# Second attention: the mask added by VectorE in the pass that finds the row maximum, instead of by a matmul

## The chip, the cores and the metric

One core of a Trainium2 chip. The time is the device time of one execution in microseconds; a lower one is better. The median of three runs stands for the kernel. Names: TensorE is PE in the rows (PEld its weight loads), VectorE is DVE, ScalarE is ACT, GpSimd is POOL, SyncE is SP.

## The reference, cut to what matters

A block of four parts on x of 16 x 256 tokens x 256: a cross attention with rotary positions, a mixture of experts, a second cross attention with a mask, and a quantised feed-forward part. The change lies in the second attention, 16 heads of 64, 256 queries and 256 keys per batch:

```python
scores = jnp.einsum('bhqd,bhkd->bhqk', q, k) / jnp.sqrt(jnp.float32(d))
scores = jnp.where(mask == 0, jnp.float32(-1000000000.0), scores)
probs = jax.nn.softmax(scores, axis=-1)
out = jnp.einsum('bhqk,bhkd->bhqd', probs, v)
```

The mask is one row of 256 keys for each query; it is the same for all heads.

## The kernel before

All parts run one after the other; the second attention (`attention1`, from L856) takes from about 1190 to 2043 us of the profile. Each engine has a program of its own, written out by hand, and semaphores join them; each engine runs its instructions in order.

**Batches and stages.** For each of the 16 batches the front makes the inputs, keys, queries and values of the batch (matmuls into the two banks pF, then high and low f16 halves: for queries and values ScalarE writes the high half, QN[0] at L1212 and VH at L1220, and VectorE the low half, L1322 and L1330; for the inputs L1205 and L1306; for keys VectorE takes the sum out of PSUM at L1315 and GpSimd splits it). The SyncE queue stacks the halves into QS, KD2 and KZ. The back works through 16 units. A unit u is a pair of heads (u // 2) and one half of the queries (u % 2), so its scores are 128 queries x 2 heads x 256 keys, one PSUM bank.

**A unit before.** TensorE (`scores`, L1133): a matmul of the identity with the mask, in bf16 and 512 columns wide, opens the bank (L1142), and four matmuls add the products of the f16 halves (L1145, L1146). VectorE (`maxima`, L1336): one reduction over the bank gives the two negated maxima NM (L1338). ScalarE (`exps`, L1225): two activations take the exponential from the bank to P32 with NM as bias, each followed by a read of its accumulator, the row sum SM (L1229). VectorE takes the reciprocal RS (L1342), GpSimd normalises P32 (L1060), TensorE transposes it (L1154) into pT, ScalarE writes the high half PH (L1238) and VectorE the low half PL (L1348), and TensorE multiplies with the values (L1167, bank pO) and with the output weights (L1179, bank pG). The output of a pair goes out of pO in halves by L1243 and L1353.

**Order.** The batch is cut into 16 turns, and a turn holds what each engine does between two units. `step` (L948) sets it: in each turn first the old batch's remainders, then the new unit's early part, then its late part, then the front of the next batch and the adding up of the experts' rows (`comb`). Lags: scores, maxima and exponentials of u in turn u, reciprocal and normalising in u + 1, transposes and halves in u + 3, the product with the values of pair p in 2p + 6, the output product in 2p + 8, the end of the batch in turn 23, that is 7 of the next. On ScalarE a turn is: high half of P (u - 3), output half, exponentials of u, then the front's item. On VectorE: maximum of u, reciprocal of u - 1, low half of u - 3, output half in even turns, then the front's item, then `comb`. The front's items come in these turns (of VectorE and ScalarE): inputs 2; keys 2, 4, 5, 6; queries 8, 9, 10, 12; values 13, 14 and 0, 1 of the next batch. In turn 0 VectorE also normalises the inputs (L1300), in turn 7 it writes the result (L1357, L1361), in 4, 6, 10 and 13 it adds experts' rows. The mask of a batch is made by GpSimd in turn 13 of the batch before (L1051).

**Buffers and waits.** Two banks pS, two pT, four P32, NM, SM and RS. Scores of u wait for the exponentials of u - 2, which free the bank (L1140); the exponentials wait for the transposes of u - 4, which free P32 (L1227); TensorE waits for the mask at unit 0 (L1136). Batches 1 to 14 run in a loop of two batches per turn (`batches`, L946), so every second batch ends at a loop wrap. The last batch has no front beside it.

Of the kernel before, what the change touches and what calls it, by code (L numbers as in the profile page):

```python
# [855 lines left out]
def attention1(nc, ctx, X, XW, ctxT_d, mask_d, bias_d, consts, POS, GW, y_d):  # L856
# [9 lines left out]
    SHRINK = float(dh) ** -0.5  # L866
    MASKED = -2.0 ** 40
# [103 lines left out]
    with nc.Block() as block:  # L971
# [35 lines left out]
        def _(pool):  # L1007
# [24 lines left out]
            def front(b, par):  # L1032
# [14 lines left out]
                def make_mask():  # L1047
                    mask_in.wait(pool, b, 16)
                    s_full.wait(pool, b, 1 - UNITS) if not isinstance(b, int) or b > 1 else None
                    nc.gpsimd.nop(nofuse=True)  # L1050
                    nc.gpsimd.tensor_scalar(maskq[par][:], maskin[:], 0.0, MASKED, ALU.is_equal, ALU.mult).then_inc(masks.sem, 1)  # L1051
# [14 lines left out]
        def _(pe):  # L1066
# [65 lines left out]
            def back(b, par):  # L1132
                def scores(u):  # L1133
                    p2, j = u // 2, u % 2
                    if u == 0:
                        masks.wait(pe, b, 1)  # L1136
                        stacked[0].wait(pe, b, 160)
                    if u == UNITS // 2:
                        stacked[1].wait(pe, b, 160)
                    e_ready.wait(pe, b, u - 1) if u or not isinstance(b, int) or b else None  # L1140
                    out = pS[u % 2]
                    nc.tensor.matmul(out[:], identb[:], maskq[par][:, j:j + 1, :].broadcast_to([P, 2, S]), start=True, stop=False)  # L1142
                    for a in range(2):
                        q = QS[par][a][:, p2, j * P:(j + 1) * P]
                        nc.tensor.matmul(out[:, a, :], q, KD2[par][a][:, p2, :], start=False, stop=False)  # L1145
                        last = nc.tensor.matmul(out[:, a, :], q, KZ[par][a][:, p2, :], start=False, stop=(a == 1))  # L1146
                    last.then_inc(s_full.sem, 1)
# [42 lines left out]
        def _(act):  # L1190
            act.wait_ge(consts_in, 64)
            nc.scalar.activation(bvh[:], bvt[:], ACT.Copy).then_inc(folds, 1)
            nc.scalar.activation(bqk[:, 0, :], bqk[:, 0, :], ACT.Copy, scale=float(dh) ** -0.5).then_inc(folds, 1)
# [30 lines left out]
            def back(b, par):  # L1224
                def exps(u):  # L1225
                    s_max.wait(act, b, u + 1)
                    t_full.wait(act, b, u - 3) if u > 2 or not isinstance(b, int) or b else None  # L1227
                    for a in range(2):
                        last = nc.scalar.activation(P32[u % 4][:, a, :], pS[u % 2][:, a, :], ACT.Exp, bias=NM[u % 4][:, a:a + 1],  # L1229
# [20 lines left out]
        def _(dve):  # L1250
# [84 lines left out]
            def back(b, par):  # L1335
                def maxima(u):  # L1336
                    s_full.wait(dve, b, u + 1)
                    nc.vector.tensor_reduce(NM[u % 4][:], pS[u % 2][:], AX.X, ALU.max, negate=True).then_inc(s_max.sem, 1)  # L1338
# [1132 lines left out]
```

## Time and profile before

| | us |
|---|---|
| median of 3 runs | 2278.15 (2271.85 to 2279.02) |
| the profiled execution | 2261.47 |
| its span, first to last instruction | 2259.8 |
| busy in it: PE / DVE / ACT / POOL | 1749.2 / 1442.3 / 1076.2 / 1019.9 |

Three views are used: busy time of the engines in a stretch, the waits (an engine's line, the line that released it, total, count and longest), and the timeline (start, duration, engine, line, output and inputs; in brackets the idle time just before and its releaser). Durations of neighbouring instructions on one engine may overlap, so the time that one holds its engine is read from the start of the next. A row with x2 is two instructions merged.

### The profile page before, as it was taken

How to read it: one execution, taken by the hardware profiler on the slowest of the kernel's cores; microseconds unless marked ns; L12 is line 12 of the kernel's file. 1: busy time of each engine (PE TensorE's matmuls, PEld its weight loads, DVE VectorE, ACT ScalarE, POOL GpSimd, SP SyncE). 2: the span in 40 equal slices, each digit the busy share in tenths (PEclk: the TensorE clock that was granted, in tenths of full speed). 3: DMA queues.
4: the chain of work that ended last, by engine and by line, in shares of the span. 5: the costliest groups of instructions: out<-in, count | busy, mean ns of one | idle time of the engine just before them, and what ended most of it. 6: DMA issues, size and time to landing. Idle time of an engine off the chain costs nothing. (4 is left out here: it accounts for less than half of the span.)

```text
span 2259.8 us, 45795 instructions
## 1 busy us (share of the span) xinstructions
PE 1749.2 (77%) x14311; PEld 1163.0 (51%) x14312; DVE 1442.3 (64%) x2962; ACT 1076.2 (48%) x2519; POOL 1019.9 (45%) x1471
## 2 busy tenths in 40 slices
PE   0588888882382689999995899999999989992375
PEld 0344444441240355666663676777666667771123
DVE  4356666666961244444444777777777777876797
ACT  1266666663520122222221666666666666671464
POOL 1655665522717102232324666665665566640005
PEclk9699999995586799999997999999999999995598
DMA  3000000003700001222213222333232222311002
GB/s 103 10 11 11 10 10 10 10 1 104 223 2 0 1 24 54 67 71 68 71 51 91 69 67 70 80 80 77 72 78 75 67 69 69 76 34 39 0 0 75
DMA packets 91476, 118.43 MB, mean 52 GB/s; under 512 B 18465, under 2 KB 60857, under 8 KB 91321
## 3 DMA queue, kind: packets, MB, share of 16 engines
q1 hardware_dynamic: 76216, 90.16, 14.9%
q0 software_dynamic: 8576, 17.87, 2.9%
q10 hardware_dynamic: 6528, 8.39, 1.1%
q8 instruction: 90, 1.47, 0.3%
q14 instruction: 66, 0.53, 0.1%
HBM read 56.40 MB, written 17.90 MB: 33 GB/s over the span
## 5 line engine op out<-in xcount | busy, mean ns | idle before, releaser
L1060 POOL TENSOR_SCALAR a_P<-a_P,a_RS 128x256 f32<-128x256 f32 x512 | 255.6, 499 | 239.1 <-DVE a_RS L1342 209.7
L1229 ACT ACTIVATE a_P<-a_pS,a_NM 128x256 f32<-128x256 f32 x512 | 237.8, 471 | 203.7 <-DVE a_NM L1338 203.2
L814 DVE TENSOR_REDUCE a_M<-a_pS 128x2 f32<-128x512 f32 x256 | 164.7, 685 | 147.1 <-PE a_pS L625 146.7
L1338 DVE TENSOR_REDUCE a_NM<-a_pS 128x2 f32<-128x512 f32 x256 | 174.7, 682 | 30.9 <-PE a_pS L1146 28.0
L1238 ACT ACTIVATE a_PH<-a_pT 128x512 f16<-128x512 f32 x256 | 154.1, 602 | 74.6 <-PE a_pT L1154 63.9
L1348 DVE TENSOR_TENSOR a_PL<-a_pT,a_PH 128x512 f16<-128x512 f32 x256 | 172.4, 673 | 13.5 <-ACT a_PH L1238 13.4
L1154 PE MATMUL a_pT<-g_ident,a_P 128*128 128x128 f32 x1024 | 156.0, 275 | 23.9 <-POOL a_P L1060 21.5
L753 ACT ACTIVATE a_PT<-a_pT 128x512 f32<-128x512 f32 x256 | 139.0, 597 | 71.6 <-PE a_pT L644 71.4
L1154 PEld LDWEIGHTS a_pT<-g_ident,a_P 128*128 128x128 f32 x1024 | 119.9, 141 | 42.5 <-POOL a_P L1060 19.4
L1921 ACT ACTIVATE me_hh<-me_pH 128x512 f16<-128x512 f32 x72 | 43.0, 597 | 175.7 <-PE me_pH L1908 156.2
L1145 PE MATMUL a_pS<-a_KD,a_QS 128*128 128x256 f16 x512 | 126.4, 274 | 0.0
L1146 PE MATMUL a_pS<-a_KZ,a_QS 128*128 128x256 f16 x512 | 126.4, 274 | 0.0
L99 PE MATMUL a_pF<-a_ch,xw_XW 128*128 128x256 f16 x512 | 100.2, 280 | 30.5 <-DVE a_VL L1330 26.6
L1966 DVE TENSOR_TENSOR me_h<-me_SG,me_pU 128x512 f32<-128x512 f32 x72 | 49.5, 688 | 98.6 <-PE me_pU L99 93.9
L99 PE MATMUL me_pG<-mo_w1h,me_xt 128*128 x288 | 98.7, 384 | 7.0 <-issue 7.0
L1229 ACT ACTIVATION_READ_ACCUMULATOR a_P<-a_pS,a_NM 128x1 f32 x512 | 102.3, 200 | 0.0
L99 PE MATMUL a_pF<-a_xh,xw_XW 128*128 128x256 f16 x512 | 99.1, 273 | 2.2 <-DVE a_k L1315 1.1
L1142 PE MATMUL a_pS<-a_maskq,g_identb 128*128 128x512 bf16 x256 | 97.8, 382 | 2.1 <-DMA a_QS<-a_QN 1.5
L99 PE MATMUL me_pU<-mo_w3h,me_xt 128*128 x288 | 98.4, 383 | 0.0
L1179 PE MATMUL a_pG<-xw_XW,a_oh 128*128 128x256 f16 x512 | 93.4, 278 | 5.5 <-DVE a_proj L1357 4.6
L1837 POOL DMA_INDIRECT me_xg<-rows,me_idx x72 | 70.3, 976 | 54.5 <-POOL me_idx L1834 34.6
L1322 DVE SCALAR_TENSOR_TENSOR a_QN<-a_pF,a_bqk,a_QN 128x256 f16<-128x256 f32 x128 | 56.0, 479 | 57.2 <-ACT a_QN L1212 44.8
(421 smaller groups left out, 5218.3 us busy)
## 6 DMA issues: line engine op xcount, KB each, us to landing
a_KD<-a_KN SPq DMA_DIRECT2D x128, 128.0 KB
a_QS<-a_QN SPq DMA_DIRECT2D x128, 128.0 KB
mr_stage<-mw SPq DMA_DIRECT2D x24, 512.0 KB, 4.7
ys<-me_yb SPq DMA_DIRECT2D x72, 128.0 KB
a_ctxin<-ctxT SPq DMA_DIRECT2D x32, 256.0 KB, 2.8
a_KZ<-a_KN SPq DMA_DIRECT2D x64, 128.0 KB
g_X<-x SPq DMA_DIRECT2D x1, 4096.0 KB, 14.8
rows<-mr_row ACTq DMA_DIRECT2D x32, 128.0 KB, 3.7
```

The costliest lines, as they stand in the source:

```text
L99: last = nc.tensor.matmul(out, a(kt), b(kt), start=(n == 0), stop=(n == 3 * chunks - 1))
L753: nc.scalar.activation(PT[(2 * p2 + a) % 8][:], pT[a][:], ACT.Exp, scale=float(dh) ** -0.5).then_inc(p_ready.sem, 1)
L814: nc.vector.reduce_max(M[:, :, a, p2], pS[a][:], AX.X).then_inc(s_max.sem, 1)
L1060: last = nc.gpsimd.tensor_scalar(P32[u % 4][:, a, :], P32[u % 4][:, a, :], RS[u % 4][:, a:a + 1], LIFT, ALU.mult, ALU.mult)
L1142: nc.tensor.matmul(out[:], identb[:], maskq[par][:, j:j + 1, :].broadcast_to([P, 2, S]), start=True, stop=False)
L1145: nc.tensor.matmul(out[:, a, :], q, KD2[par][a][:, p2, :], start=False, stop=False)
L1146: last = nc.tensor.matmul(out[:, a, :], q, KZ[par][a][:, p2, :], start=False, stop=(a == 1))
L1154: last = nc.tensor.transpose(pT[u % 2][:, a, kt, :], P32[u % 4][:, a, kt * P:(kt + 1) * P], ident[:])
L1229: last = nc.scalar.activation(P32[u % 4][:, a, :], pS[u % 2][:, a, :], ACT.Exp, bias=NM[u % 4][:, a:a + 1], accum_out=SM[u % 4][:, a:a + 1])
L1238: nc.scalar.activation(PH[p2 % 2][:, :, :, j * P:(j + 1) * P].rearrange("p a k q -> p (a k) q"), pT[u % 2][:].rearrange("p a k q -> p (a k ...
L1338: nc.vector.tensor_reduce(NM[u % 4][:], pS[u % 2][:], AX.X, ALU.max, negate=True).then_inc(s_max.sem, 1)
L1348: nc.vector.tensor_tensor(PL[p2 % 2][:, :, :, j * P:(j + 1) * P].rearrange(f), pT[u % 2][:].rearrange(f), PH[p2 % 2][:, :, :, j * P:(j + 1 ...
```

## The change

TensorE no longer adds the mask; the first product opens the bank. The sign of the scaled queries is turned (SHRINK, and the scale of their bias), so the bank holds negated scores, and the mask is +2^40 where it was -2^40. VectorE runs one `tensor_tensor_reduce` for each of the two heads of a unit: it adds the mask to 256 columns of the bank, writes the sum to P32 and its minimum, which is the negated maximum of the scores, to NM. ScalarE reads P32 and writes the exponentials over it, with a scale of -1. The bank is free when the second pass is done, so the scores of u wait for the maxima of u - 2. The waits for the mask and for P32 go to VectorE, which gets a no-operation that carries them. GpSimd's wait before it overwrites a mask goes by the maxima.

```diff
-    SHRINK = float(dh) ** -0.5
-    MASKED = -2.0 ** 40
+    SHRINK = -float(dh) ** -0.5
+    MASKED = 2.0 ** 40
...
                 def make_mask():
                     mask_in.wait(pool, b, 16)
-                    s_full.wait(pool, b, 1 - UNITS) if not isinstance(b, int) or b > 1 else None
+                    s_max.wait(pool, b, -UNITS) if not isinstance(b, int) or b > 1 else None
...
                 def scores(u):
                     p2, j = u // 2, u % 2
                     if u == 0:
-                        masks.wait(pe, b, 1)
                         stacked[0].wait(pe, b, 160)
                     if u == UNITS // 2:
                         stacked[1].wait(pe, b, 160)
-                    e_ready.wait(pe, b, u - 1) if u or not isinstance(b, int) or b else None
+                    s_max.wait(pe, b, u - 1) if u or not isinstance(b, int) or b else None
                     out = pS[u % 2]
-                    nc.tensor.matmul(out[:], identb[:], maskq[par][:, j:j + 1, :].broadcast_to([P, 2, S]), start=True, stop=False)
                     for a in range(2):
                         q = QS[par][a][:, p2, j * P:(j + 1) * P]
-                        nc.tensor.matmul(out[:, a, :], q, KD2[par][a][:, p2, :], start=False, stop=False)
+                        nc.tensor.matmul(out[:, a, :], q, KD2[par][a][:, p2, :], start=(a == 0), stop=False)
...
-            nc.scalar.activation(bqk[:, 0, :], bqk[:, 0, :], ACT.Copy, scale=float(dh) ** -0.5).then_inc(folds, 1)
+            nc.scalar.activation(bqk[:, 0, :], bqk[:, 0, :], ACT.Copy, scale=-float(dh) ** -0.5).then_inc(folds, 1)
...
                 def exps(u):
                     s_max.wait(act, b, u + 1)
-                    t_full.wait(act, b, u - 3) if u > 2 or not isinstance(b, int) or b else None
                     for a in range(2):
-                        last = nc.scalar.activation(P32[u % 4][:, a, :], pS[u % 2][:, a, :], ACT.Exp, bias=NM[u % 4][:, a:a + 1],
+                        last = nc.scalar.activation(P32[u % 4][:, a, :], P32[u % 4][:, a, :], ACT.Exp, bias=NM[u % 4][:, a:a + 1], scale=-1.0,
                                                     accum_out=SM[u % 4][:, a:a + 1])
...
                 def maxima(u):
                     s_full.wait(dve, b, u + 1)
-                    nc.vector.tensor_reduce(NM[u % 4][:], pS[u % 2][:], AX.X, ALU.max, negate=True).then_inc(s_max.sem, 1)
+                    if u == 0:
+                        masks.wait(dve, b, 1)
+                    t_full.wait(dve, b, u - 3) if u > 2 or not isinstance(b, int) or b else None
+                    nc.vector.nop(nofuse=True)
+                    for a in range(2):
+                        last = nc.vector.tensor_tensor_reduce(P32[u % 4][:, a, :], pS[u % 2][:, a, :], maskq[par][:, u % 2, :], 1.0, 3.0e38,
+                                                              ALU.add, ALU.min, NM[u % 4][:, a:a + 1])
+                    last.then_inc(s_max.sem, 1)
```

## Rows read from the trace of the kernel before

**Rows 1.** Busy us (and counts) of PE, PEld, DVE, ACT, POOL; clock, DMA share, GB/s.
```profile
1340.00:1940.00 600.00, 551.74 (x4847) 422.47 (x4846) 468.71 (x1101) 381.86 (x1193) 367.46 (x563) 0.99 0.30 73
```

**Rows 2.** Waits in 1340 to 1940 us: total us, times, longest.
```profile
ACT a_P L1229 <- DVE a_NM L1338: 159.0, 150, 2.1
...
DVE a_VL L1330 <- ACT a_VH L1220: 36.2, 46, 1.0
DVE a_QN L1322 <- ACT a_QN L1212: 33.6, 35, 1.2
...
DVE a_NM L1338 <- PE a_pS L1146: 21.1, 17, 2.5
...
PE a_pF L99 <- DVE a_VL L1330: 20.9, 12, 2.2
```

**Rows 3.** Timeline of DVE, turn 9 of a batch.
```profile
1677.11 0.68 DVE L1338 TENSOR_REDUCE a_NM<-a_pS 128x2 f32<-128x512 f32 x1
1677.71 0.15 DVE L1342 RECIPROCAL a_RS<-a_SM 128x2 f32<-128x2 f32 x1
1677.78 0.67 DVE L1348 TENSOR_TENSOR a_PL<-a_pT,a_PH 128x512 f16<-128x512 f32 x1
1679.61 0.88 DVE L1322 SCALAR_TENSOR_TENSOR a_QN<-a_pF,a_bqk,a_QN 128x256 f16<-128x256 f32 x2 [1.16 <-ACT a_QN L1212]
1680.40 0.68 DVE L1338 TENSOR_REDUCE a_NM<-a_pS 128x2 f32<-128x512 f32 x1
```

**Rows 4.** Timeline of ACT in the same turn.
```profile
1677.82 0.48 ACT L1229 ACTIVATE a_P<-a_pS,a_NM 128x256 f32<-128x256 f32 x1 [0.87 <-DVE a_NM L1338]
1678.19 0.19 ACT L1229 ACTIVATION_READ_ACCUMULATOR a_P<-a_pS,a_NM 128x1 f32 x1
...
1678.64 0.20 ACT L1229 ACTIVATION_READ_ACCUMULATOR a_P<-a_pS,a_NM 128x1 f32 x1
1678.74 0.84 ACT L1212 ACTIVATE a_QN<-a_pF,a_bqk 128x256 f16<-128x256 f32 x2
```

**Rows 5.** Timeline of PE: mask matmul and the next one; a resumption at a loop wrap.
```profile
1657.00 0.38 PE L1142 MATMUL a_pS<-a_maskq,g_identb 128*128 128x512 bf16 x1
1657.22 0.27 PE L1145 MATMUL a_pS<-a_KD,a_QS 128*128 128x256 f16 x1
...
1696.36 1.02 PE L1154 MATMUL a_pT<-g_ident,a_P 128*128 128x128 f32 x4 [2.38 <-POOL a_P L1060]
```

**Rows 6.** Timeline of DVE, turns 4 to 6.
```profile
1661.59 0.69 DVE L1338 TENSOR_REDUCE a_NM<-a_pS 128x2 f32<-128x512 f32 x1 [1.07 <-PE a_pS L1146]
...
1662.66 0.69 DVE L1348 TENSOR_TENSOR a_PL<-a_pT,a_PH 128x512 f16<-128x512 f32 x1 [0.30 <-ACT a_PH L1238]
1663.27 0.41 DVE L1353 SCALAR_TENSOR_TENSOR a_ol<-a_pO,a_oh 128x256 f16<-128x256 f32 x1
1663.60 0.87 DVE L1315 TENSOR_SCALAR a_k<-a_pF,a_bqk 128x256 f32<-128x256 f32 x2
...
1669.02 0.88 DVE L1315 TENSOR_SCALAR a_k<-a_pF,a_bqk 128x256 f32<-128x256 f32 x2 [0.53 <-PE a_pF L99]
```

**Rows 7.** Timeline of DVE: the maxima of turn 11 and of turn 13.
```profile
1684.08 0.68 DVE L1338 TENSOR_REDUCE a_NM<-a_pS 128x2 f32<-128x512 f32 x1
...
1689.04 0.68 DVE L1338 TENSOR_REDUCE a_NM<-a_pS 128x2 f32<-128x512 f32 x1
```

**Rows 8.** Groups by line, 1340 to 1940 us: busy us, mean ns; idle time before.
```profile
L1201 ACT ACTIVATE a_ch<-a_ctxin 128x512 f16<-128x512 f32 x12 | 7.7, 639 | 0.0
L1205 ACT ACTIVATE a_xh<-a_pF 128x512 f16<-128x512 f32 x12 | 7.1, 593 | 0.0
```

**Rows 9.** The maxima: ns min/median/max, first and last start; turn 0 of two batches.
```profile
L1338 DVE TENSOR_REDUCE a_NM<-a_pS x256: 670/680/693, 1240.2 to 2032.7; 128x2 f32<-128x512 f32 x128
...
1700.81 0.69 DVE L1338 TENSOR_REDUCE a_NM<-a_pS 128x2 f32<-128x512 f32 x1 [2.37 <-PE a_pS L1146]
...
1751.25 0.69 DVE L1338 TENSOR_REDUCE a_NM<-a_pS 128x2 f32<-128x512 f32 x1
```

## The prediction

> **What bounds the kernel now.** I read the windows first: in 1340 to 1940 us, the middle of the second attention, TensorE is busy 551.7 of 600 us, VectorE 468.7, ScalarE 381.9, GpSimd 367.5 [rows 1]. Taken alone that says TensorE is the bound, and taking a matmul from it should pay. So the next view was who waits for whom [rows 2]. TensorE's gaps end with VectorE's work (L1330, 20.9 us in 12 waits), while VectorE waits for ScalarE (36.2 us for VH, 33.6 us for QN) and ScalarE for VectorE's maxima (159.0 us). VectorE waits for TensorE's scores only 21.1 us in 17 waits. Two engines that wait for each other on every turn are a loop, so I read their timelines through one turn.
>
> A turn is one unit u of the program. In turn 9, VectorE finds the maximum at 1677.11, takes the reciprocal and the low half of P, and then stands idle 1.16 us until ScalarE has the high half of the queries; at 1679.61 it takes the low half and at 1680.40 the next maximum [rows 3]. ScalarE starts the exponentials at 1677.82, 0.71 after the maximum began; they and the two accumulator reads take 0.92, and QN follows at 1678.74 with no gap [rows 4]. The turn is 0.71 + 0.92 + 0.87 (QN with the hand-over) + 0.79 = 3.29 us, and 1680.40 - 1677.11 is 3.29. TensorE is not in that loop. By the plans, eight of the sixteen turns of a batch have a ScalarE item of the front (inputs, queries or values) that VectorE must follow and are of this kind: 0, 1, 2, 8, 9, 10, 13, 14. Turns 11 and 12 are one loop too: 4.96 us from maximum to maximum with two sets of exponentials in it [rows 7]. Turns 5, 6, 7 and 15 are filled by VectorE itself, apart from 0.53 us at L1315. Turns 3 and 4 hang on TensorE: the maximum waits 1.07 us for the scores, L1348 then 0.30 us for the transposes [rows 6]. A batch without a loop wrap is 50.4 us (1751.25 - 1700.81) [rows 9].
>
> **The change, part by part** (per batch of 16 units; 15 batches run with a front beside them).
>
> Mask matmul gone: the next matmul starts 0.22 us after it [rows 5], so TensorE gets 16 x 0.22 = 3.5 us back per batch. It counts only where TensorE is what the loop waits for: once in turns 3 and 4 (-0.22).
>
> Maximum in two passes. Now one pass starts the next instruction 0.60 us later (1677.11 to 1677.71) and lasts 0.68 [rows 3, 9]. The new operation isn't in the trace. Its nearest pass is L1353, 128x256 from PSUM with an immediate: 0.41 us long, next instruction 0.33 after its start [rows 6]. It also writes out its minimum. VectorE shows no such write; its nearest row is the reciprocal of 128x2, which lasts 0.15 and lets the next start after 0.07 [rows 3]. I take these, with 0.08 for the second figure: the engine is held 2 x (0.33 + 0.08) = 0.82 us, +0.22 against 0.60; the result is there after 0.33 + 0.08 + 0.33 + 0.15 = 0.89 us, +0.21 against 0.68. Low end: no cost for the minimum, 0.33 + 0.41 = 0.74 (+0.06), engine +0.06. High end: nothing overlaps, the minimum costs ScalarE's 0.20 and the no-operation that carries the waits 0.07, so 0.07 + 2 x (0.41 + 0.20) = 1.29 (+0.61), engine +0.7. I take the middle values because they come from the same engine's own rows.
>
> The Trainium skill (VectorE: DVE Perf Modes, section "Two Vector instructions with no wait between them") says that an operation which writes its accumulator is two instructions, and its Vector Engine (DVE) Microarchitecture Reference, section 5.2, gives 1.04 ns per column and some 75 ns per instruction after overlap. Estimated from that page alone, the four would hold the engine 0.83 us. No run here shows it yet.
>
> Exponentials from SBUF: ScalarE's 128x512 copy takes 0.639 us from SBUF (L1201) and 0.593 from PSUM (L1205) [rows 8], +0.046 per instruction, +0.09 per unit. The sign in the scale is an immediate and free.
>
> Bank free earlier (scores wait for the maximum of u-2, not its exponentials): worth nothing, TensorE hardly waits there; the cover is that it reaches scores after its own queue. Waits moved to VectorE: t_full of u-4 stands in TensorE's queue ahead of scores u, so it has passed when s_full has; the mask is made on GpSimd in turn 13, three turns ahead. Behind a wait there would queue the reciprocal, the low half and all front items, and behind them TensorE; I see none that lasts. GpSimd's mask instruction is the same; negated queries cost nothing.
>
> **The sum.** The eight loop turns: each +0.21 + 0.09 = +0.30, 2.40. Turns 11 and 12: +0.21 and twice 0.09, +0.39. Turns 7 and 15, VectorE full: +0.22 each, 0.44. Turns 5 and 6: twice 0.22, less the 0.53 wait at L1315 that fills up, as TensorE is now early: -0.09. Turns 3 and 4: -0.22; VectorE's longer pass fits in its 1.07 us wait. Together +2.92 us per batch, x15 = +43.8. At some wraps of the batch loop TensorE resumes late (2.38 us of idle time) and VectorE's maximum then waits 2.37 us for it [rows 5, 9]; there turns 14 and 15 give and take nothing. Of the 17 waits of 21.1 us [rows 2], 12 are turn 4's 1.07, and the 8.3 us left are some four such wraps: -2. The last batch has no front and is set by TensorE at one place and VectorE at the next: 0. **+42 us.** The profiled execution took 2261.5 us around a span of 2259.8, below the three runs shown (2271.9 to 2279.0). On its own time the sum gives 2303.5; on the median of 2278.15 it gives **2320**, which I forecast.
>
> Same sum with the low ends: 8 x 0.15 + 0.24 + 0.12 - 0.41 - 0.22 = +0.9 per batch, +14 us, 2292. With the high ends: 8 x 0.70 + 0.8 + 1.4 + 0.9 + 0.1 = +8.8, +132 us, 2410.
>
> **Rivals.** *TensorE is the bound* (the other side): at 92% busy, with the matmul's time coming back on every unit, 256 x 0.22 = 56 us less, 2222. It decides if in turns 8 to 14 TensorE's queries or values were what ScalarE waits for. Against it: QN starts the moment the exponentials end [rows 4], and TensorE is found waiting for VectorE and GpSimd [rows 2]. The Trainium skill (Trainium Kernel Development and Optimization, section "Performance Expectations") calls matmul busy time a bad metric for how close a kernel is to its limit; by that rule the trace agrees, its 92% standing beside those waits. Chance 0.08. If TensorE bounded part of the turns only, some gain would be left after the VectorE cost.
>
> *The passes overlap wholly*, and an early TensorE also cures part of the stalls at the wraps: +14 less some 10, within 0.3% (2271.3 to 2285.0, about what a measurement of this kernel can tell from no change). Chance 0.08.
>
> *The passes run one after the other*, each waiting for its minimum: VectorE goes from 39.1 us per 50 (468.7 of 600) [rows 1] to over 50 and is the bound in every turn: up to 2410. For it: an unseen operation, on 512 instructions; against it: all VectorE rows overlap by 0.07 to 0.09. Chance 0.2.
>
> *The change doesn't do what it says* in one point: the bank is released earlier, and nobody was waiting for it. That is in the forecast already and has no chance of its own. The forecast itself has 0.64.
>
> **Numbers.** Slower: 0.64 + 0.20, so 0.84; same 0.08; faster 0.08. The range leaves out the faster rival and the upper half of the serial one: 2286 to 2362.
>
> **What would show it.** Right: no L1142; two passes of 0.40 to 0.45 us per unit with a second row each; exponentials some 0.05 us longer; VectorE busy up by about 3.5 us per batch; turn 9 at 3.6 us; ScalarE still waits for NM in most units; TensorE busy near 85% and its waits for VectorE and GpSimd up. Its granted clock, 0.99 in the window [rows 1], could fall with longer gaps, which would add to the time. Wrong: if turn 9 stays at 3.29, the passes are cheaper than any row says; if the batch falls below 50 us, TensorE was in the loop; if t_full or the mask shows up as a releaser of VectorE, the moved waits are not free.

## The result and the profile after

| | us |
|---|---|
| before, median of 4 runs | 2275.0 (2269.6 to 2279.0) |
| after, median of 4 runs | 2312.26 (2307.6 to 2320.5) |
| ratio, with its 95% interval | 1.0169 [1.0131, 1.0208] |
| span of the profiled execution, before / after | 2259.8 / 2310.4 |

The change costs 37 us by the medians; 42 were forecast. To see where the time went, I took the starts of the maxima of all 256 units from VectorE's timeline in both traces; from one start to the next is a turn. Over the 15 batches that have a front beside them, the turns add up to +41.7 us, against a forecast of +43.8 - 2. The two profiled spans differ by more, 50.6 us; 7.6 of that lies behind the last maximum, nearly all in work that the change doesn't touch, and over all the traces of this case that tail takes 227 to 239 us with and without the change. The batch loop has five wraps: it runs batches 1 to 12 in six passes of two, and the last batches stand behind it. Sorted by turn:

| turns, 15 batches | forecast | after | what it is |
|---|---|---|---|
| 8 to 14 | +28.4 | +16.3 | loop turns, and 11 with 12 |
| 0 to 7 | +12.2 | +8.1 | loop turns 0 to 2; 3 to 6; 7 |
| 15, no wrap behind it | +3.3, with wraps | +5.4 | end of a batch |
| 15, at the 5 wraps | -2 | +11.8 | loop wraps |

(The forecast's figures are its per-batch terms times 15: 8 to 14 are five turns of 0.30 and the 0.39; 0 to 7 are 0.90 - 0.22 - 0.09 + 0.22.) The total is right because two errors nearly cancel: the turns grew by less than forecast, and the wraps of the batch loop grew where I had a small gain.

The busy window that answers to [rows 1], with the same columns:

```profile
1340.00:1940.00 600.00, 508.11 (x4372) 386.37 (x4372) 462.45 (x1568) 371.40 (x1128) 344.22 (x531) 0.96 0.28 69
```

TensorE has gone from 551.7 to 508.1 us of 600, and the kernel is slower. VectorE's busy time even fell in the window, for the window now holds less of the work; in it its instructions rose from 1101 to 1568. The granted clock fell from 0.99 to 0.96.

The page's groups and the source view of the new line show its price; the columns are busy us, mean ns, idle time before, and then ns min/median/max with the first and last start:

```profile
L1340 DVE CUSTOM_DVE_ANT_0 a_P<-a_pS,a_maskq 128x256 f32<-128x256 f32 x512 | 194.9, 417 | 49.9 <-PE a_pS L1144 44.9
```

```profile
L1340 DVE DVE_READ_ACCUMULATOR2_ANT a_NM<- x512: 72/82/86, 1241.3 to 2076.4; 128x1 f32 x171
```

Turn 9 on VectorE, which answers to [rows 3]:

```profile
1701.33 0.41 DVE L1340 CUSTOM_DVE_ANT_0 a_P<-a_pS,a_maskq 128x256 f32<-128x256 f32 x1
1701.67 0.08 DVE L1340 DVE_READ_ACCUMULATOR2_ANT a_NM<- 128x1 f32 x1
1701.67 0.42 DVE L1340 CUSTOM_DVE_ANT_0 a_P<-a_pS,a_maskq 128x256 f32<-128x256 f32 x1
1702.01 0.08 DVE L1340 DVE_READ_ACCUMULATOR2_ANT a_NM<- 128x1 f32 x1
1702.01 0.16 DVE L1346 RECIPROCAL a_RS<-a_SM 128x2 f32<-128x2 f32 x1
...
1703.98 0.88 DVE L1319 SCALAR_TENSOR_TENSOR a_QN<-a_pF,a_bqk,a_QN 128x256 f16<-128x256 f32 x2 [1.22 <-ACT a_QN L1210]
1704.77 0.41 DVE L1340 CUSTOM_DVE_ANT_0 a_P<-a_pS,a_maskq 128x256 f32<-128x256 f32 x1
```

Read the starts. The read of the minimum and the second pass both start at 1701.67, the second read and the reciprocal both at 1702.01: the read takes no time of its own from the engine. The two passes hold it 0.68 us (1701.33 to 1702.01), against 0.60 for the one before. The turn is 1704.77 - 1701.33 = 3.44, against 3.29.

ScalarE in the same turn, answering to [rows 4]:

```profile
1702.13 0.51 ACT L1226 ACTIVATE a_P<-a_P,a_NM 128x256 f32<-128x256 f32 x1 [1.14 <-DVE a_NM L1340]
1702.55 0.19 ACT L1226 ACTIVATION_READ_ACCUMULATOR a_P<-a_P,a_NM 128x1 f32 x1
1702.64 0.49 ACT L1226 ACTIVATE a_P<-a_P,a_NM 128x256 f32<-128x256 f32 x1
...
1703.13 0.81 ACT L1210 ACTIVATE a_QN<-a_pF,a_bqk 128x256 f16<-128x256 f32 x2
```

The exponentials start 0.80 after the maximum (0.71 before) and take 1.00 until QN (0.92 before); QN with the hand-over takes 0.85 (0.87), and VectorE's QN 0.79 (0.79). So 0.80 + 1.00 + 0.85 + 0.79 = 3.44. The loop is the one that the prediction read out, with two terms longer by 0.09 and 0.08.

Waits in the same window, answering to [rows 2]:

```profile
ACT a_P L1226 <- DVE a_NM L1340: 188.1, 142, 2.7
...
PE a_pT L1152 <- POOL a_P L1060: 56.0, 51, 2.9
...
DVE a_QN L1319 <- ACT a_QN L1210: 43.4, 44, 1.2
DVE a_P L1340 <- PE a_pS L1144: 36.5, 24, 4.0
DVE a_VL L1327 <- ACT a_VH L1218: 36.3, 45, 1.0
```

TensorE's time went into waiting: it waits 56.0 us for normalised P. New, though, is VectorE's wait for scores, up from 21.1 us to 36.5, with single waits of up to 4.0 us. The longest, 3.86 to 3.99 us, stand at the five loop wraps. TensorE's timeline and VectorE's at the wrap before the batch of 1727.59:

```profile
1724.98 0.27 PE L1144 MATMUL a_pS<-a_KZ,a_QS 128*128 128x256 f16 x1
```

```profile
1723.56 0.16 DVE L1287 TENSOR_TENSOR a_rstd<-a_root,a_corr 128x2 f32<-128x2 f32 x1
1727.59 0.42 DVE L1340 CUSTOM_DVE_ANT_0 a_P<-a_pS,a_maskq 128x256 f32<-128x256 f32 x1 [3.86 <-PE a_pS L1144]
```

The last product of unit 0's scores ends at 1725.25, and VectorE starts on them at 1727.59, 2.3 us later (0.8 to 3.3 us at the five wraps). The wait is put down to TensorE because that signal is the last one the profile shows; but TensorE had been done. Before, at the wrap of [rows 9], VectorE's maximum started right behind the scores. Turn 15 before a wrap is now 6.19, 6.26, 6.15, 6.14 and 6.18 us, where it was 4.67, 4.29, 2.69, 4.54 and 2.94. The spread of before follows TensorE's granted clock: in the 4 us ahead of the maximum it is 0.57, 0.58 and 0.61 at the three long wraps (the lower of the two levels, 1.2 GHz, reads 0.50), and 1.00 at the two short ones:

```profile
1696.81:1700.81 4.00, 4.00 (x27) 2.54 (x26) 1.53 (x8) 1.89 (x6) 0.96 (x2) 0.61 0.04 10
1798.32:1802.32 4.00, 2.88 (x28) 2.19 (x29) 2.68 (x8) 1.92 (x6) 1.83 (x4) 1.00 0.13 45
```

Against those two, a wrap has grown by 3.4 us, not by the 2.4 of the mean.

### The profile page after: what moved, and what is told of

It is laid out like the page before. It is cut to its first block and busy times, and to the rows that moved or that the text cites. A ratio compares the mean times of both kernels' runs of the same rounds, so it can differ in the third digit from the quotient of the medians.

```text
span 2310.4 us, 46083 instructions
## 1 busy us (share of the span) xinstructions
PE 1741.2 (75%) x14047; PEld 1152.3 (50%) x14056; DVE 1467.7 (64%) x3730; ACT 1092.3 (47%) x2519; POOL 1018.6 (44%) x1471
## 5 line engine op out<-in xcount | busy, mean ns | idle before, releaser
L1226 ACT ACTIVATE a_P<-a_P,a_NM 128x256 f32<-128x256 f32 x512 | 255.7, 500 | 254.4 <-DVE a_NM L1340 252.2
L1340 DVE CUSTOM_DVE_ANT_0 a_P<-a_pS,a_maskq 128x256 f32<-128x256 f32 x512 | 194.9, 417 | 49.9 <-PE a_pS L1144 44.9
L1152 PE MATMUL a_pT<-g_ident,a_P 128*128 128x128 f32 x1024 | 163.1, 283 | 74.0 <-POOL a_P L1060 69.7
L99 PE MATMUL a_pF<-a_ch,xw_XW 128*128 128x256 f16 x512 | 105.1, 289 | 37.4 <-DVE a_VL L1327 31.7
L1226 ACT ACTIVATION_READ_ACCUMULATOR a_P<-a_P,a_NM 128x1 f32 x512 | 95.7, 187 | 0.0
L1573 POOL DMA_INDIRECT slots<-ms_tok,g_POS x64 | 61.9, 967 | 61.6 <-DVE g_POS L1711 42.4
```

The costliest lines, as they stand in the source:

```text
L99: last = nc.tensor.matmul(out, a(kt), b(kt), start=(n == 0), stop=(n == 3 * chunks - 1))
L1152: last = nc.tensor.transpose(pT[u % 2][:, a, kt, :], P32[u % 4][:, a, kt * P:(kt + 1) * P], ident[:])
L1226: last = nc.scalar.activation(P32[u % 4][:, a, :], P32[u % 4][:, a, :], ACT.Exp, bias=NM[u % 4][:, a:a + 1], scale=-1.0, accum_out=SM[u % ...
L1340: last = nc.vector.tensor_tensor_reduce(P32[u % 4][:, a, :], pS[u % 2][:, a, :], maskq[par][:, u % 2, :], 1.0, 3.0e38, ALU.add, ALU.min, N ...
```

## The experiments

Three theories were at stake. *Loop*: the turns are set by the VectorE-ScalarE loop, and grow by the pass and by the source. *TensorE*: its time matters too, through its idle gaps or its clock. *Restart*: VectorE comes back late at a wrap because of what its program has become. All ratios are against runs of the kernel before on the same chip.

### TensorE's time alone: the mask matmul taken out

```diff
-                        masks.wait(pe, b, 1)
-                    nc.tensor.matmul(out[:], identb[:], maskq[par][:, j:j + 1, :].broadcast_to([P, 2, S]), start=True, stop=False)
-                        nc.tensor.matmul(out[:, a, :], q, KD2[par][a][:, p2, :], start=False, stop=False)
+                        nc.tensor.matmul(out[:, a, :], q, KD2[par][a][:, p2, :], start=(a == 0), stop=False)
```

The mask isn't applied.

> The kernel before with the mask matmul left out and nothing put in its place (the mask is not applied). The loop theory (VectorE's maximum, ScalarE's exponentials and high half, VectorE's low half, next maximum set the turn; TensorE only waits): turn 9 stays at 3.29 us and the maxima of a batch stay near 50.4 us; between 10 us less and 15 us more than before, that is 2265 to 2290. More is possible where TensorE, done sooner, idles longer at the end of a batch and its clock is granted low after it, which the changed kernel shows (2.41 us idle at 1667.19, then matmuls 0.21 us apart where they are 0.11 apart elsewhere). The TensorE theory: 256 x 0.22 us less, 2219.

Measured: 2268.46 us, ratio 0.999 [0.9977, 1.0003]. The window:

```profile
1340.00:1940.00 600.00, 529.86 (x4634) 404.54 (x4635) 471.71 (x1098) 379.48 (x1192) 366.64 (x565) 0.97 0.29 72
```

TensorE has 22 us less in 600, and the time is the same; turn 9 stays at 3.29. Turn 3 is mostly 2.20 for 2.41, the 0.22 that was forecast for turns 3 and 4, but three batches have 3.14 to 3.18 there, with a granted clock of 0.80 to 0.88 in that turn, and the five wraps add next to nothing either way (3.96 in the mean, before 3.83). The rival in which TensorE is the bound is dead.

### The other way round: a blank matmul put into the changed kernel

```diff
+    blank = s.sb("blank", [P, 1, S], BF16)
...
+                    nc.tensor.matmul(out[:], identb[:], blank[:, 0:1, :].broadcast_to([P, 2, S]), start=True, stop=False)
```

> The changed kernel with a matmul of the same width as the mask's, identity times a tile of zeros, put back in front of the products (it adds zero). The loop theory: TensorE has the time to spare; its idle gap before turn 0 shortens and its clock stays high there, so 0 to 10 us less than the changed kernel, 2302 to 2312. The TensorE theory: 56 us more than the changed kernel, 2368.

Measured: 2314.6, ratio 1.0208 [1.0186, 1.0231]; the change itself has 1.0169 [1.0131, 1.0208]. Turn 9 is 3.44, and turn 15 at the wraps 6.18, 6.37, 6.45, 6.15 and 6.15: giving TensorE its old load back cures nothing. So the long wraps don't come from a TensorE that is less busy. Nor do they come from its clock: at the third and fourth of these wraps it is 1.00 in the 4 us ahead of the maximum, as it is at all five of the fourth experiment (6.55 to 6.81 us). The 0 to 10 us less that I expected didn't come either: the turns add up to 7.9 us more than with the change, 7.3 of them in turns 0 to 7, where turn 3 takes 3.2 to 3.7 us in seven batches.

### The waits and the no-operation alone

```diff
                     s_full.wait(dve, b, u + 1)
+                    if u == 0:
+                        masks.wait(dve, b, 1)
+                    t_full.wait(dve, b, u - 3) if u > 2 or not isinstance(b, int) or b else None
+                    nc.vector.nop(nofuse=True)
                     nc.vector.tensor_reduce(NM[u % 4][:], pS[u % 2][:], AX.X, ALU.max, negate=True).then_inc(s_max.sem, 1)
```

> The kernel before with only the three things that the change puts in front of the maxima on VectorE: the wait for the mask at unit 0, the wait for the transposes of u-4, and the no-operation. In the changed kernel VectorE restarts 3.9 us after its last instruction at each of the five wraps of the batch loop (turn 15 takes 6.2 us where it took 2.7 to 4.7), and turns 7 and 13, where VectorE waits for itself, are longer by 0.27. If the added instructions do this: turn 15 at the wraps goes to some 5 to 6 us, turns 7 and 13 up by 0.1 to 0.2, 10 to 20 us more than before, 2285 to 2295. If they are free and the wraps come from TensorE's clock or from the passes: 2275 within 5.

Measured: 2275.33, ratio 1.0029 [1.0014, 1.0044]. Turns 8 and 9 stay at 3.30 and 3.29, so in a loop turn the waits are free. They are not where short instructions stand ahead of the maximum: turn 6 is 4.39 for 4.19, turn 13 4.45 for 4.35 and turn 15 2.54 for 2.31. Turns 0 to 7 carry +8.8 us of the turns' sum of +8.7, and the wraps, at 2.95 to 3.24 us, give 3.8 back. In both of these figures TensorE's clock has a part. Turn 3 is 2.51 for 2.41, but 3.2 to 3.7 in five batches, and in three of them turn 2 is longer too, 6.0 us together; there the granted clock falls to 0.50 for some 2 us in turns 2 and 3, behind an idle gap of TensorE of 2.0 to 2.2 us that other batches have at the full clock, while it reads 1.00 in those turns of before in every batch but the first. At the wraps it is the other way round: all five have 1.00 here, and three of before had 0.57 to 0.61, some 5 us. The two nearly cancel, so that moving the waits costs some 7 us in all (2275.33 against 2268.3), a term that I had at nothing. Whether the waits also bring on the low clock isn't shown; three batches of the first experiment have it in turn 3 without them. The opposite, the change without these waits or the no-operation, wasn't tried.

### The maximum ahead of the front's item, in every turn

If the loop sets the turns, taking its hinge out should pay: VectorE takes the maximum of u + 1 before it waits for ScalarE's half of QN or VH.

```diff
-                return {}, plan(*[(u, lambda u=u: maxima(u)) for u in range(UNITS)], ...
+                return {}, plan((0, lambda: maxima(0)), ...
+                            *[(u - 1, lambda u=u: maxima(u)) for u in range(1, UNITS)], (END, finish))
```

> The changed kernel with VectorE's two passes of unit u+1 put in front of the front's item of turn u instead of behind it (turns 1 to 15), so that ScalarE can go from the high half straight to the next exponentials. The loop theory: the loop is cut; ScalarE's own work per turn is 2.1 to 2.5 us and TensorE's 2.7, so turn 9 falls from 3.44 to under 3 and a batch from 53 to 45 to 48 us: 2200 to 2250. The TensorE theory, and the theory that VectorE's own work bounds the changed kernel: the order of VectorE's queue moves nothing, 2312 within 10.

Measured: 2310.73, ratio 1.0203 [1.0169, 1.0238]. No gain in the total, where 2200 to 2250 was expected, though turn 9 falls to 2.14. Turns 8 to 15 take 24.1 us for 26.2, but turns 0 to 7 take 27.7 for 26.2, and a wrap 6.7. The waits show what replaced the loop where it hadn't been the limit:

```profile
DVE a_P L1340 <- PE a_pS L1144: 119.1, 102, 3.2
POOL a_KN L1043 <- DVE a_k L1312: 61.5, 22, 4.3
```

In turns 0 to 7 VectorE now stands in front of scores that aren't there yet, with the keys' item queued behind it, on which GpSimd waits. The order pays in the late turns only.

### The maximum ahead in six turns only, without and with the change

```diff
+    EARLY = (9, 10, 11, 13, 14, 15)
...
-                return {}, plan(*[(u, lambda u=u: maxima(u)) for u in range(UNITS)], ...
+                return {}, plan(*[(u, lambda u=u: maxima(u)) for u in range(UNITS) if u not in EARLY], ...
+                            *[(u - 1, lambda u=u: maxima(u)) for u in EARLY], (END, finish))
```

> The kernel before with the maxima of units 9, 10, 11, 13, 14 and 15 put in front of the front's item of the turn ahead, so that the loop is cut in the turns of the queries and values alone. In the run that moved all maxima, turns 0 to 7 became longer (27.7 us where the changed kernel has 26.2: its keys hang on VectorE) and turns 8 to 15 shorter (24.1 against 26.2). The loop theory: turns 8 to 15 fall from 25.2 to 23 to 24.5 us per batch and the rest stays, 10 to 30 us less than before, 2240 to 2260. If TensorE is at its bound there: nothing, 2268.

> The same order in the changed kernel. The loop theory: turns 8 to 15 near the 24.1 us of the full reorder, turns 0 to 7 near 26.2, so 2 us per batch or 30 us less than the changed kernel, 2275 to 2290, the wraps still near 6 us. If the changed kernel is bound by the number of its VectorE instructions: 2312 within 8.

Measured: the kernel before, reordered, 2236.15, ratio 0.9862 [0.9838, 0.9885]; the changed one, reordered, 2240.5, ratio 0.9881 [0.9859, 0.9903]. The first one's window:

```profile
1340.00:1940.00 600.00, 568.07 (x5038) 437.26 (x5037) 484.61 (x1147) 403.21 (x1245) 383.48 (x585) 1.00 0.30 75
```

This shows the loop: not one instruction is taken away, turn 9 falls from 3.29 to 2.05, and every engine is busier. (A single turn now overstates it, since the starts of the maxima have moved: outside the wraps turns 8 to 15 together fall from 24.6 to 23.0 us.) With the loop cut, the two ratios lie within each other's intervals. The changed kernel came out below the 2275 to 2290 expected, because that expectation took turns 8 to 15 from the run that had moved all maxima; moving six gives 21.8 us there and not 24.1. Outside the wraps the turns of the changed one are 42.3 us shorter than those of the kernel before, and of the unchanged one 33.4: the longer pass and the slower source cost nothing there any more. What is left of the change's price is in the wraps, 7.26, 6.94, 8.00, 6.75 and 8.50 us with it, 4.48 to 5.01 without; this is more than the 6 us expected, and why they grew with the new order is open (at the 8.00 and the 8.50 the scores end only 0.3 us before VectorE takes them, with a granted clock of 0.60 and 0.50 ahead of them).

### One pass for both heads

```diff
-                    for a in range(2):
-                        last = nc.vector.tensor_tensor_reduce(P32[u % 4][:, a, :], pS[u % 2][:, a, :], ...
+                    last = nc.vector.tensor_tensor_reduce(P32[u % 4][:], pS[u % 2][:], maskq[par][:, u % 2:u % 2 + 1, :].broadcast_to([P, 2, S]), 1.0, 3.0e38,
+                                                          ALU.add, ALU.min, NM[u % 4][:, 0:1])
```

Both heads share one minimum, which ScalarE takes as the bias of both.

> The changed kernel with one 512-column tensor_tensor_reduce per unit in place of two of 256: both heads of a unit share one minimum, the larger of the two maxima, which the softmax divides out again. The mask's broadcast to two heads and the sums to P32 stay. Half the custom instructions and accumulator reads: the engine is held some 0.6 instead of 0.69 us and the minimum is there after some 0.68 to 0.76. Theory that the custom instructions lengthen the restart of VectorE at the five wraps (6.2 us of turn 15): it falls to 3 to 5 us, and the loop turns by 0.08 to 3.36: 15 to 25 us less than the changed kernel, 2287 to 2297. Theory that the low TensorE clock after the idle gap makes the wraps long: turn 15 stays above 6, 8 to 12 us less from the loop turns alone, 2300 to 2304.

Measured: 2293.59, ratio 1.0104 [1.0061, 1.0148]. The group, and VectorE at a wrap:

```profile
L1339 DVE CUSTOM_DVE_ANT_1 a_P<-a_pS,a_maskq 128x512 f32<-128x512 f32 x181 | 123.6, 683 | 37.1 <-issue 16.9 <-PE a_pS L1144 15.2 <-DVE a_bn L1271 2.3
```

```profile
1715.16 0.16 DVE L1287 TENSOR_TENSOR a_rstd<-a_root,a_corr 128x2 f32<-128x2 f32 x1
1718.67 0.69 DVE L1339 CUSTOM_DVE_ANT_1 a_P<-a_pS,a_maskq 128x512 f32<-128x512 f32 x1 [3.34 <-issue]
```

One pass of 512 columns takes 0.683 us, as long as the reduction it replaces (0.680, [rows 9]): adding the mask on the way is free, and cutting the pass in two costs 0.08. Turn 9 is 3.36 for 3.44. At the wraps (5.54 to 5.64 us) the idle time now has no releaser but "issue": nothing that the profile shows was missing, and VectorE still stood for 3.34 us. That is the restart, seen without another name on it. The time came out as the theory of the custom instructions had it (2287 to 2297), but not its mechanism, which had the wraps at 3 to 5 us: halving their number shortened a wrap by only 0.6.

### The exponentials read from the bank

```diff
-                    s_max.wait(pe, b, u - 1) if u or not isinstance(b, int) or b else None
+                    e_ready.wait(pe, b, u - 1) if u or not isinstance(b, int) or b else None
...
-                        last = nc.scalar.activation(P32[u % 4][:, a, :], P32[u % 4][:, a, :], ACT.Exp, ...
+                        last = nc.scalar.activation(P32[u % 4][:, a, :], pS[u % 2][:, a, :], ACT.Exp, ...
```

VectorE still does its passes and writes P32, but the exponentials lack the mask.

> The changed kernel with the exponentials read from the PSUM bank instead of P32 (so the mask is not applied), and the scores waiting for the exponentials of u-2 again. It takes away the SBUF source alone. ScalarE's 128x256 activation goes from 0.500 back to 0.47 us, and the nine or so turns in which it stands in the loop lose what it adds there: turn 9 from 3.44 to 3.37, 7 to 12 us less than the changed kernel, 2300 to 2305. If the source costs nothing in the loop and the passes make up all of its 0.15: 2312 within 4 and turn 9 at 3.44.

Measured: 2298.22, ratio 1.0143 [1.0115, 1.017]. The activations of this kernel, then of the change:

```profile
L1226 ACT ACTIVATE a_P<-a_pS,a_NM 128x256 f32<-128x256 f32 x358 | 166.5, 471 | 193.0 <-DVE a_NM L1340 191.6
```

```profile
L1226 ACT ACTIVATE a_P<-a_P,a_NM 128x256 f32<-128x256 f32 x354 | 176.8, 500 | 189.6 <-DVE a_NM L1340 188.1
```

0.471 us from PSUM, 0.500 from SBUF, and turn 9 is 3.37 for 3.44: the source costs 0.07 a turn. The turns add up to 10.2 us less than with the change, where 7 to 12 were expected; by the ratios it is 6 us, with overlapping intervals, so the sum over the kernel is less sure than the turn. The wraps stay at 6.1 to 6.3, and the bank, which scores again wait longer for, shows no cost in the turns.

### Two built-in reductions in place of one

Is it the new operation, or the number of instructions, that makes the wraps long?

```diff
+                    nc.vector.nop(nofuse=True)
+                    for a in range(2):
+                        last = nc.vector.tensor_reduce(NM[u % 4][:, a:a + 1], pS[u % 2][:, a, :], AX.X, ALU.max, negate=True)
+                    last.then_inc(s_max.sem, 1)
```

This is the kernel before, mask matmul and all, with the waits of the third experiment as well.

> The kernel before with the added waits and the no-operation on VectorE, and its one reduction split in two of 256 columns: as many VectorE instructions per unit as the changed kernel has, but built-in ones, and the mask still on TensorE. Theory that the tensor_tensor_reduce operations themselves make VectorE restart late at the wraps: turn 15 at the five wraps stays near the 3.0 us of the run with the waits alone, and turn 9 goes to 3.37 (the split adds the same 0.08 as the two passes), 2268 + 7 for the waits + 12 for eight or nine longer turns in 15 batches = 2280 to 2290. Theory that the count of instructions does: turn 15 at the wraps 5 to 6 us and 2290 to 2300.

Measured: 2301.03, ratio 1.0138 [1.01, 1.0177]. Turn 9 is 3.35, and VectorE at a wrap:

```profile
1389.84 0.16 DVE L1290 TENSOR_TENSOR a_rstd<-a_root,a_corr 128x2 f32<-128x2 f32 x1
1393.43 0.76 DVE L1343 TENSOR_REDUCE a_NM<-a_pS 128x1 f32<-128x256 f32 x2 [3.43 <-issue]
```

The wraps are 5.67, 5.56, 5.75, 5.55 and 5.66. The third experiment has the same waits and 3.0. One plain reduction more per unit, with the waits in place, makes the restart long; the mask, the new operation, SBUF as a source and TensorE's load are all as they were before. Most of the change's cost, 0.0138 of 0.0169 with overlapping intervals, comes with two instructions and their waits in place of one.

### The batch loop written out

```diff
-        with eng.Fori(0, B // 2 - 2) as i:
+        for i in range(B // 2 - 2):
```

> The changed kernel with the loop over the batches of the second attention written out, so that no engine but SyncE's queue branches back there. If the wraps cost what turn 15 shows (6.2 us against 2.7 elsewhere, five times): 15 to 20 us less than the changed kernel, 2292 to 2297, and no turn 15 above 3.5. If the late restarts come from the batch boundary and not from the branch, or if a longer program has to be fetched just as late: 2312 within 6, with late restarts in other places.

Measured: 2284.09, ratio 1.0064 [1.0044, 1.0084], with the change otherwise as it is. That is 24 us less than the change by the ratios, more than the 15 to 20 expected. Without the wraps turn 15 is 2.45 in most batches and 3.1 to 3.4 in five, which are the ones with a granted clock of 0.76 in the 7 us around the end of the batch; the others have 1.00. Turn 7 falls from 3.06 to 2.75. Turns 8 to 14 together are +15.7 us over before, as with the loop (+16.3). How much of the 24 us between the ratios the kernel before would also gain by this edit wasn't run; its own wraps leave 5 x (3.83 - 2.31) = 7.6 us to be had, and the reordered one gains 3 to 4 by it, within its interval (below).

The profile has two queues that bring instructions, and one of them, q14, shows the other side. Its row, packets, MB and share of the DMA engines, in 1340 to 1940 us of the change, of the two built-in reductions and of the change written out:

```profile
q14 instruction: 59, 0.48, 0.3%
```

```profile
q14 instruction: 53, 0.43, 0.2%
```

```profile
q14 instruction: 32, 0.26, 0.1%
```

The kernel before has 30 and the waits alone 30; one pass, with its one read, has 55. In the 7 us around the wrap that starts the batch of 1727.59, this queue brings 5 packets of 8 KB; around the wrap of [rows 9] before it brings 2. Wherever the body of the loop has grown by one or more VectorE instructions per unit, beside the waits and the no-operation, these packets come in about twice the number (53 to 61) and the wraps are 5.5 us or longer; where it is written out, neither. The other queue, q8 with packets of 16 KB, doesn't go with the wraps: it brings 51 packets with the waits alone and 49 with the two built-in reductions, 24 without the mask matmul and 22 with the change. The Trainium skill (Runtime: NRT & Kernel Launch, section "Instruction fetch mechanics") says that an engine's instructions are brought ahead in order, and that a taken branch to a place outside what is held must be fetched before the engine goes on. By that rule, the rows agree: idle time with no releaser right behind a backward branch, and instruction packets in it. That the packets of q14 are VectorE's is not in any row, and from which size of the body on it happens wasn't tried.

### The loop cut and the wraps gone

> The reordered kernel before, with the same loop written out. Its turn 15 at the wraps is 4.8 us on average against 3.67: 5 to 8 us less than its 2236, 2228 to 2231. If code cannot be fetched in time: more than 2236.

> The reordered changed kernel with the same loop written out. Its turn 15 at the wraps is 7.5 us on average against 3.28, and its other batches take 48.0 us where the reordered kernel before has 48.6. If the wraps are all that keeps it behind: 20 us less than its 2240, 2218 to 2224, which is less than the reordered kernel before in either form, since with the loop of VectorE and ScalarE cut the 0.22 us per unit on TensorE count. If code cannot be fetched in time: 2235 or more.

Both put the order of the six turns and the written-out loop together. Measured: without the change 2233.12, ratio 0.9845 [0.9823, 0.9867]; with it 2225.45, ratio 0.9805 [0.9785, 0.9825]. A batch is 48.33 us without (1577.42 to 1625.75) and 47.73 with (1579.92 to 1627.65), steady over the batches; 0.6 us over the 13 that repeat is 7.8 us, and the medians differ by 7.7. That these agree so closely is partly chance: the profiled execution with the change is the slowest of its four (2233.21) and the other the fastest of its four (2227.83), the difference lying outside the second attention, and the two intervals just overlap. Both times are a little above what was expected (2228 to 2231, 2218 to 2224). With both obstacles gone the same change is a gain of some 0.4%, plain in the attention's turns and at the edge of the noise in the whole time, and this kernel is the fastest of all, 2.0% below the one before. Its window:

```profile
1340.00:1940.00 600.00, 543.79 (x4975) 429.16 (x4974) 520.67 (x1781) 423.75 (x1274) 392.87 (x603) 1.00 0.31 76
```

TensorE works 544 us of 600 at full clock; VectorE, at 521, has been given the most.

## Why the prediction was right, and where it was wrong

**What bounds the kernel: right.** The loop of four terms in turn 9 was named, and it is that: TensorE's time was worth nothing (first experiment), moving VectorE's maximum ahead in six turns of 16 was worth 1.4% (the reordered kernel before), and both longer terms of the change show up in it one for one. The rival *TensorE is the bound* (0.08, 2222) fell, and with it the 56 us that a count of busy time promised.

**The pass: mechanism right, size wrong.** The step was "the engine is held 2 x (0.33 + 0.08)", +0.22, and the result +0.21 late. The pass is 0.417 us with 0.34 to the next, as taken from L1353. But the read of the minimum costs the engine nothing: the next pass starts with it. Measured +0.08 on the engine and +0.09 for the result, close to the low end (+0.06), which was "no cost for the minimum". The row I took instead, the reciprocal, is an operation of its own that reads and writes; a read of the accumulator on the same engine was nowhere in the trace of before, so the middle value had no better ground than the low end. The rival in which the passes run one after the other (0.2, up to 2410) fell for the same reason. The Trainium skill's rule that such an operation is two instructions (VectorE: DVE Perf Modes, section "Two Vector instructions with no wait between them") agrees with the rows, which list both. The estimate of 0.83 us of engine time that the prediction made from the skill's per-instruction figure does not agree: measured 0.68. It is 0.15 too high, which is what it charges for the two reads. Of the other signs named, VectorE's busy time rose by 25 us (1442.3 to 1467.7), 1.6 a batch and not 3.5, turn 9 is 3.44 and not 3.6, and TensorE is at 85% (508.1 of 600), as forecast.

**The source: right.** +0.09 a turn forecast, +0.07 measured, and 0.029 per activation where the copies of [rows 8] showed 0.046.

**Turns.** A loop turn grew by 0.15 and not 0.30, and that carries turns 8 to 14: half of 28.4 would be 14.2, and 16.3 were measured; most of the rest is turn 13, which the moved waits alone make 0.10 longer (third experiment), 1.5 us over 15 batches. Turns 0 and 1 grew by only 0.07 to 0.08, not by the pass and the source together. I counted them as loop turns because they have a values item. With the exponentials read from the bank they are back at 4.47 and 2.94, with the two built-in reductions they are at 4.52 and 3.00, so either alone can give this growth and the two don't add; why is open. Turns 3 and 4 lose the 0.22 in ten batches, as forecast (2.41 + 3.19 to 2.33 + 3.05), and give it back in five, where turn 3 is 3.0 to 3.2: in these the granted clock reads 0.50 for part of turns 2 and 3, and 1.00 in the other batches but the first. Turn 7 has +0.27, near the forecast 0.22, but only 0.09 of it is the pass; the rest is L1365, which takes 0.916 us where the same line took 0.757. The waits alone leave it at 0.754, the two built-in reductions make it 0.974, and written out it is 0.751 and the turn 2.75. So it needs the loop, but the longer body alone doesn't bring it: with all maxima moved, as long a body and wraps of 6.7 us, it is 0.761. By what way it comes is open.

**The moved waits: wrong.** "I see none that lasts" is true, since neither the mask nor t_full shows up as a releaser of VectorE's pass, and the waits still cost: 0.29% by the third experiment. It shows in turns 6, 13 and 15, where short instructions stand ahead of the maximum (+0.20, +0.10, +0.23).

**The wraps: wrong, in sign.** The step was "at some wraps TensorE resumes late ... there turns 14 and 15 give and take nothing", and then -2 us. Measured +11.8 at the five wraps. I read the 2.37 us ahead of a maximum as TensorE's lateness, which it was in that trace, and priced only what changes for TensorE (the 8.3 us of waits that I gave to some four wraps are those of all five, and the -2 had no working); that VectorE's own program gets longer, and that it comes back late from a backward branch for that, was no term of the sum. This cost hangs on the loop and not on the work in it: the wraps are 6.2 us with the change, 3.0 with the waits alone, 5.6 with one more plain instruction, and gone when the loop is written out.

**The clock: named, not priced.** "Its granted clock could fall with longer gaps." At the end of a batch in the middle of the loop body TensorE now idles 2.41 us before its transposes, where it idled 1.42 before. In some batches it then goes on at the lower of its two levels, 1.2 GHz, the products of pO 0.21 us apart for 0.11, and in others, behind the same gap, it doesn't:

```profile
1667.19 1.11 PE L1152 MATMUL a_pT<-g_ident,a_P 128*128 128x128 f32 x4 [2.41 <-POOL a_P L1060]
1668.23 0.42 PE L1165 MATMUL a_pO<-a_PH,a_VH 128*64 128x256 f16 x2
1668.45 0.42 PE L1165 MATMUL a_pO<-a_PL,a_VH 128*64 128x256 f16 x2
...
1776.69 0.66 PE L1152 MATMUL a_pT<-g_ident,a_P 128*128 128x128 f32 x4 [2.41 <-POOL a_P L1060]
1777.27 0.30 PE L1165 MATMUL a_pO<-a_PH,a_VH 128*64 128x256 f16 x2
```

The same place in the kernel before:

```profile
1748.08 0.66 PE L1154 MATMUL a_pT<-g_ident,a_P 128*128 128x128 f32 x4 [1.42 <-POOL a_P L1060]
1748.67 0.30 PE L1167 MATMUL a_pO<-a_PH,a_VH 128*64 128x256 f16 x2
```

The two stretches of the change, in the view of [rows 1]:

```profile
1665.40:1672.40 7.00, 5.21 (x33) 3.45 (x34) 5.22 (x24) 4.09 (x13) 2.65 (x5) 0.76 0.14 42
1774.28:1781.28 7.00, 4.59 (x40) 3.41 (x41) 5.74 (x26) 4.08 (x13) 2.66 (x5) 1.00 0.21 64
```

Turn 15 is 3.30 us in the first and 2.68 in the second. Of the ten batch ends without a wrap, three with the full clock take 2.67 or 2.68, and four with a granted clock of 0.76 take 3.05 to 3.41; the first two and the last take 2.82, 2.83 and 2.03. So some 2.5 us of the +5.4 are the clock's in this execution; of the growth that is left, from 2.31 to 2.67, the waits alone account for 0.23. In the kernel before all ten have 1.00 in the same 7 us.

In sum: forecast 2320 with 0.84 for slower, measured 2312. The verdict and the bound stand on the mechanism; the closeness of the number is luck, two errors of opposite sign: about -16 us in the turns and +16 in turn 15 and the wraps. The size of the second depends on the execution too, since three of the five wraps of before were long by TensorE's clock.

## What to carry to other kernels

Time a turn from one instruction's start to its next start, and write it as a sum over the engines it passes through; what an edit is worth is what it does to those terms, and here an engine with 92% busy time, outside the sum, was worth nothing. When two in-order engines hold each other, move an instruction in one queue first and price other changes after that: here the same change cost 1.7% before and gained some 0.4% once the order and the loop wraps were out of the way. Where an engine's program gets longer inside a loop, look at the idle time right behind the wrap on that engine, and test the written-out loop.

## What the hardware showed that I had not expected

- `tensor_tensor_reduce` with a bf16 mask on a 128x512 f32 bank takes 0.683 us, the plain reduction of the same bank 0.680. Its accumulator read (0.082 us) costs the engine nothing.
- VectorE stood 3.3 to 4.2 us at a loop wrap (up to 5.6 in the reordered changed kernel), with the change 0.8 to 3.3 of it after its scores were there, once its loop body had one or more instructions more per unit; packets of instruction queue q14 in 600 us went from 30 to between 53 and 61.
- Waits and a no-operation behind short VectorE instructions added 0.10 to 0.23 us to the turn (13 and 15), and nothing where the engine had been waiting anyway.
- An idle gap of 2.41 us on TensorE at the end of a batch was followed by products at the lower level in some batches and at the full clock in others, so the length of the gap alone does not decide it here; in the kernel before, gaps of 1.42 us were never followed by the lower level. The lower level added 0.4 to 0.7 us to that turn.
